# Self attention's last steps: low parts of the first context's tiles ahead of y's statistics, and four splits of W_kvc three steps later

## The chip, the cores and the metric

The kernel runs on one core of one Trainium2 chip. TensorE (PE), VectorE (DVE), ScalarE (ACT), GpSimd (POOL) and SyncE (SP) each work through an instruction stream of their own and meet at semaphores. The metric is the device time of one execution in microseconds (us); the median of several executions is compared.

## The reference, cut to what matters

It is one transformer block with cross attention, for 16 batches of 224 tokens of width 512 in 16 heads, and a context of 750 tokens for each batch:

```python
qkv = modulate(_ln(x), shift_a, scale_a) @ W_qkv + b_qkv
x = x + gate_a[:, None] * (softmax(q @ k^T * scale) @ v) @ W_proj + b_proj   # self attention, gate on all of the projection
q_c = _ln(x) @ W_qc + b_qc
kv_c = _ln(context) @ W_kvc + b_kvc
k_c, v_c = jnp.split(kv_c, 2, axis=-1)
x = x + (softmax(q_c @ k_c^T * scale) @ v_c) @ W_cproj + b_cproj             # cross attention
x = x + gate_m[:, None] * mlp(modulate(_ln(x), shift_m, scale_m))
```

(The attention lines are abridged: heads, transposes and the place of the bias are left out.)

## The kernel before, in words

Three phases follow each other: self attention (up to about 764 us of the profiled execution), cross attention (to about 1.8 ms) and the MLP. A product with full precision is made of three products of halves: every operand is split into a high part (rounded, `_h`) and a low part (the rest, `_l`), and `product` (lines 72 to 74) multiplies low by high, high by low and high by high. A split so takes two instructions: ACT writes the high part (a copy that rounds), and then DVE subtracts it from the source to get the low part.

Self attention is a software pipeline. `bodies` calls each engine's `body` for batches 0 to 16 (16 only drains what is left), and in each body `h` runs over 16 steps. Each engine has its own list of work for a step, written out by hand in the order in which the lines of its loop stand. Nothing is scheduled at run time: an engine takes its instructions in that order and waits at each semaphore that isn't there yet. PE's step has scores of one head (`score`, and `score_t` of the head six steps back), then fill work (projections for other batches), then P.V and its sums (`pv`, `sums`) and transposes (`turn_x`, `turn_y`, `turn_context`).

The last 32 steps, counted by `seam_step(b, h) = (b.c - 15) * 16 + h` (0 to 15 are batch 15's, 16 to 31 the drain's; NH is 16), also start the cross attention of its first batch, so that PE has work:

- `load_wkv` loads the weight W_kvc in eight chunks of 128x512 (four for v, four for k). `high_wkv(i)` on ACT (line 1101, tile cross_wkv_h) and `low_wkv(i)` on DVE (line 873, tile cross_wkv_l) split chunk i, ACT one step ahead of DVE. The steps are in the table `WKV_AT`.
- The context of batch 0 is six tiles of 125 tokens. At the steps of `TILES_AT` PE turns tile t (`turn_context`, line 702), ACT writes its high part (`high_context`, line 1113) and DVE its low part (`low_context`, line 895, tile cross_cT_l).
- `cross_v(t)` on PE at the steps `V_AT` (15 to 20) multiplies tile t with the v half of W_kvc. It waits for the low part of its tile, and for the four v chunks.
- `cross_k(i)` at the steps `K_AT` makes k. The first is at step 21 (NH + 5), in bank sc_ps, and begins with

```python
if i == 0:
    pe.wait_ge(wkv_l, 2 * KC)
```

  so it waits for the low parts of all eight chunks.
- The end of self attention goes on besides: `stats` (line 821, bn_stats of y), `rstd` on POOL (lines 1279 and 1281), `neg_mean` (line 831) and `apply_ln` on ACT (line 1096) normalize y, the residual sum; `turn_y` on PE (line 563), `highs_y` on ACT (line 1171) and `low_y` on DVE (line 866, tile self_yT_l) turn and split it. `turn_y` of batch 14 stands at steps 20 and 21, at the end of PE's step. `stats_context` (line 877) on DVE makes the statistics of the second context at step 19, and `sum_p` on POOL (line 1294) adds the two halves of each head's exponentials.

Self attention ends in a barrier (line 99): the cross phase starts on each engine when all have come to it.

Of the kernel before, what the change touches and what calls it, by code (L numbers as in the profile page):

```python
# [23 lines left out]
NH, HD = 16, 32  # L24
# [139 lines left out]
def self_phase(nc, x, cond_t, w_mod, b_mod, w_qkv, b_qkv_t, w_proj, b_proj, w_qc, b_qc_t, gates, x1, qc, mod_t,  # L164
# [3 lines left out]
    with ExitStack() as ctx:  # L168
# [143 lines left out]
        INVERSE_AT, MEAN_AT = (6, NH + 5), (7, NH + 7)  # L312
        NORMAL_AT = ({7: (0,), 8: (1,), 9: (2,), 10: (3,), 11: (4, 5)}, {NH + 11: (0, 1, 2), NH + 12: (3, 4, 5)})
        TILES_AT = {12: (0,), 13: (1,), 14: (2, 3), 15: (4, 5)}
        WKV_AT = (9, 10, 11, 12, 14, 15, NH, NH + 1)
        V_AT = {15: 0, NH: 1, NH + 1: 2, NH + 2: 3, NH + 3: 4, NH + 4: 5}
        K_AT = {NH + 5: 0, NH + 7: 1, NH + 8: 2, NH + 12: 3, NH + 13: 4, NH + 14: 5, NH + 15: 6}
        KEEP_K_AT = {NH + 6: 0, NH + 9: 1, NH + 10: 2, NH + 12: 3, NH + 13: 4, NH + 14: 5, NH + 15: 6}
# [5 lines left out]
        def seam_step(b, h):  # L324

            return (b.c - (B - 1)) * NH + h

        def early_division(step):

            return step >= -2 and step != 2  # L330
# [8 lines left out]
        def fills(b, h, kinds):  # L339
            if b.c in END:  # L340
                return [(kind, c, part, Batch(o)) for kind, c, part, o in END[b.c][h] if kind in kinds]
            return [(*f, b.plus(of(f))) for f in FILL[h] if f[0] in kinds and exists(b, f)]
# [19 lines left out]
        def tile_bank(o, t):  # L362

            return (st_ps + sc_ps)[t % 4] if o else pj_ps[t % 2]
# [452 lines left out]
        def _(dve):  # L817
# [11 lines left out]
            def neg_mean(b, mv, rs, nm, s_rstd, s_nmr):  # L829
                dve.wait_ge(s_rstd, b.n(1, 1))  # L830
                dve.scalar_tensor_tensor(out=nm[:], in0=mv[:, :, 0], scalar=-1.0, in1=rs[:], op0=ALU.mult, op1=ALU.mult).then_inc(s_nmr, 1)
# [58 lines left out]
            def low_context(o, t):  # L890
                at = slice(t * SN, (t + 1) * SN)
                if o == 0 and t == 0:
                    dve.wait_ge(turned, NH * (B - 1))
                dve.wait_ge(seam.cT_h, o * ST + t + 1)
                dve.tensor_tensor(seam.cT[1][:, :, at], tile_bank(o, t)[:, 0:KC * SN].rearrange("p (k n) -> p k n", k=KC),
                                  seam.cT[0][:, :, at].bitcast(F32), ALU.subtract).then_inc(seam.cT_l, 1)
# [15 lines left out]
            def split_maxima(b, g):  # L912
                turned = tx_ps[0:HPG * QT, 0:QN]
                dve.wait_ge(m_ps, b.n(KC, g + 1))
                wait(dve, m_in, b.n(32 * KC, 32 * g))
                dve.tensor_copy(mrow[0][:], turned).then_inc(m_h, 1)
                dve.wait_ge(m_h, b.n(KC, g + 1))
                dve.tensor_tensor(mrow[1][:], turned, mrow[0][:].bitcast(F32), ALU.subtract).then_inc(m_row, 1)
# [9 lines left out]
            def evict(kind, c, part, o):  # L928
                if kind == "k" and part == 1:
                    lows(o, c, k_h, k_l, bqkv, KC + 2 * c, nat)  # L930
                if kind == "q" and part == 1:
                    lows(o, c, q_h, q_l, bqs, 2 * c, natq)
                if kind == "c" and part == 1:
                    lows(o, c, c_h, c_l, bqcs, 2 * c, natq)
                if kind == "p" and part == 1:
                    add_bias(o, c)

            def body(b, att, nxt, prv, old):
                z, y2, far_b = b.plus(-1), b.plus(-2), b.plus(2)
                for h in range(NH):  # L940
                    if h % HPG == HPG - 1 and att:
                        split_maxima(b, h // HPG)
                    for f in fills(b, h, "kqcpv")[0:1]:
                        evict(*f)
                    if h < NH - 1 and att:
                        row_max(b, h + 1)
                    if h == NH - 1 and nxt:
                        row_max(b.plus(1), 0)
                    for f in fills(b, h, "kqcpv")[1:]:
                        evict(*f)  # L950
                    for _, c, _, o in fills(b, h, ("tx",)):
                        modulate(o, c)
                    for _, c, _, o in fills(b, h, ("ty",)):
                        low_y(o, c)
                    for back in (1, 2):
                        for o, g in late_group(b, h - back, att, prv) if early_division(seam_step(b, h - back)) == (back == 1) else ():
                            normalize(o, g)
                    if h == 14 and att:
                        low_o(b, 0)
                    if h in LOW_O and prv:  # L960
                        low_o(z, LOW_O[h])
                    if seam_step(b, h) in KEEP_K_AT:
                        low_k(KEEP_K_AT[seam_step(b, h)])
                    if far(b) and h == 6:
                        stats(far_b, x_in, x_loaded, lambda t: far_b.n(16, 0), st1, mv1, stats1, mvs1)
                    if far(b) and h == 8:
                        neg_mean(far_b, mv1, rs1, nm1, rstd1, nmr1)
                    if prv and h == (12 if b.c == B else 15):
                        stats(z, y, summed, lambda t: z.n(2, t + 1), st2, mv2, stats2, mvs2)
                    if old and h == 0:  # L970
                        neg_mean(y2, mv2, rs2, nm2, rstd2, nmr2)
                    if b.c == B and h == 13:
                        neg_mean(z, mv2, rs2, nm2, rstd2, nmr2)
                    if b.c == 0 and 2 <= h < 2 + KC:
                        low_w(3 * KC + h - 2)
                    if b.c == 1 and h == 0:
                        gate_rows(3)
                    if b.c == 1 and h in (13, 14):
                        mlp_row(h - 9)
                    if b.c == 1 and h == 15:  # L980
                        keep_modulation()
                    if b.c == 2 and 5 <= h < 5 + KC:
                        low_w(4 * KC + h - 5)
                    if seam_step(b, h) in WKV_AT:
                        low_wkv(WKV_AT.index(seam_step(b, h)))
                    for t in TILES_AT.get(seam_step(b, h), ()):
                        low_context(0, t)
                    for o in range(2):
                        for t in STATS_AT[o].get(seam_step(b, h), ()):
                            stats_context(o, t)  # L990
                        if seam_step(b, h) == max(STATS_AT[o]):
                            aggregate_context(o)
                        if seam_step(b, h) == MEAN_AT[o]:
                            neg_mean_context(o)
# [98 lines left out]
        def _(act):  # L1093
# [103 lines left out]
            def body(b, att, nxt, prv, old):  # L1197
                z, y2 = b.plus(-1), b.plus(-2)
                for h in range(NH):
# [28 lines left out]
                    for t in TILES_AT.get(seam_step(b, h), ()):  # L1228
                        high_context(0, t)
                    if seam_step(b, h) + 1 in WKV_AT:  # L1230
                        high_wkv(WKV_AT.index(seam_step(b, h) + 1))
                    if seam_step(b, h) == NH:
# [1554 lines left out]
```

## Time and profile before

| | |
|---|---|
| Time, median of 3 executions | 2610.44 us (2610.37 to 2615.86) |
| Profiled execution, its own time | 2611.72 us |
| Its span on the profile | 2609.9 us |
| PE busy | 2571.6 us, 99% of the span |
| DVE busy | 1695.0 us, 65% |
| ACT busy | 1127.6 us, 43% |
| POOL busy | 1274.4 us, 49% |

The span is what the profile covers; the execution's own time is 1.8 us longer. A matmul's row in the profile lasts longer than the matmul keeps its successor waiting, since matmuls are pipelined: how fast PE works is read from the distance between the starts of two matmuls, not from their durations. The same holds in small for DVE and ACT, whose rows overlap the next by some 0.08 us.

### The profile page before, as it was taken

To read this page: it belongs to the slowest core of one execution; us is meant where nothing else is said; L and a number is where in the kernel's file an instruction comes from. 1 tells how busy PE (TensorE), PEld (TensorE's weight loads), DVE (VectorE), ACT (ScalarE), POOL (GpSimd) and SP (SyncE) were. 2 spreads that over 40 slices of the span, in tenths; PEclk is the share of its full clock that TensorE was granted. 3 is DMA by queue.
4 is the path that set the end of the run, shared out by engine and by line. 5 is a ranking of instruction groups with operands and counts; after the bars stand their busy time and mean duration, and the time that the engine had idled before them with its cause. 6 is when DMAs were issued, how large, how long until landed. Compare 5 with 4: busy or idle time off the path is not lost.

```text
span 2609.9 us, 50236 instructions
## 1 busy us (share of the span) xinstructions
PE 2571.6 (99%) x18696; PEld 2127.4 (82%) x18696; DVE 1695.0 (65%) x3399; ACT 1127.6 (43%) x2192; POOL 1274.4 (49%) x1426
## 2 busy tenths in 40 slices
PE   8999999999899999999999999999899999999999
PEld 6688888888788888888888888887678888888887
DVE  6677777777767777777777777776764444444442
ACT  4354454444535555555555555554542222212111
POOL 1445454454536777777777777775421121220230
PEclk9999999999999999999999999999899999999999
DMA  7554545555554444444444444433521111111110
GB/s 224 133 134 125 136 120 131 129 125 133 146 147 114 122 107 118 112 111 117 112 117 108 123 117 109 122 95 101 150 93 45 37 45 34 44 49 37 45 53 17
DMA packets 193045, 269.89 MB, mean 103 GB/s; under 512 B 34788, under 2 KB 112612, under 8 KB 192788
## 3 DMA queue, kind: packets, MB, share of 16 engines
q1 hardware_dynamic: 187116, 254.16, 36.9%
q0 software_dynamic: 3264, 7.92, 0.9%
q10 hardware_dynamic: 2424, 4.61, 0.7%
q8 instruction: 150, 2.46, 0.4%
q14 instruction: 91, 0.75, 0.1%
HBM read 111.11 MB, written 36.77 MB: 57 GB/s over the span
## 4 chain that ended last, share of the span: by engine, by line
PE 69%; DVE 1%; issue 0%; DMA 0%; ACT 0%; SPq 0%; DVEq 0%; ACTq 0%
PE late_sc_ps L1782 7%; PE late_or_ps L1811 5%; PE late_even_ps L72 5%; PE late_sc_ps L72 5%; PE late_even_ps L73 5%; PE late_even_ps L74 5%; PE late_sc_ps L74 5%; PE late_sc_ps L73 5%; PE shared_tr_ps L1798 4%; PE late_odd_ps L72 3%; PE late_odd_ps L74 3%; PE late_odd_ps L73 3%; PE late_tr_ps L1798 3%; PE late_odd_ps L1743 1%; PE late_tr_ps L72 1%; PE late_tr_ps L74 1%
## 5 line engine op out<-in xcount | busy, mean ns | idle before, releaser
L1970 DVE TENSOR_REDUCE cross_parts<-late_sc_ps 112x1 f32<-112x500 f32 x512 | 335.5, 663 | 219.3 <-PE late_sc_ps L1782 218.3
L2224 POOL TENSOR_TENSOR cross_part<-cross_prT 125x448 f32<-125x448 f32 x232 | 271.6, 1171 | 214.6 <-ACT cross_prT L2148 177.2
L1294 POOL TENSOR_TENSOR self_psum<-self_prT 112x224 f32<-112x224 f32 x256 | 178.3, 697 | 327.4 <-ACT self_prT L1160 318.3
L2626 ACT ACTIVATE mlp_hv<-late_sc_ps,mlp_b 128x512 f32<-128x512 f32 x112 | 77.2, 689 | 511.3 <-PE late_sc_ps L74 496.9
L2148 ACT ACTIVATE cross_prT<-shared_tr_ps 125x448 f32<-125x448 f32 x379 | 206.5, 545 | 164.3 <-PE shared_tr_ps L1798 158.3
L2226 POOL TENSOR_TENSOR cross_part<-cross_part,cross_prT 125x448 f32<-125x448 f32 x232 | 268.1, 1156 | 18.2
L1782 PE MATMUL late_sc_ps<-cross_kst,cross_qst 96*112 96x500 f32 (+1 forms) x1024 | 261.2, 336 | 3.5 <-DVE cross_parts L1970 1.7
L2148 ACT ACTIVATE cross_prT<-late_tr_ps 125x448 f32<-125x448 f32 x380 | 206.8, 544 | 109.4 <-PE late_tr_ps L1798 106.6
L2540 DVE CAST mlp_hT_h<-mlp_hv 128x512 fp32r<-128x512 f32 x112 | 57.0, 509 | 300.1 <-ACT mlp_hv L2626 300.1
L1160 ACT ACTIVATE self_prT<-self_st_ps 112x448 f32<-112x448 f32 x256 | 138.6, 542 | 167.3 <-PE self_st_ps L629 165.7
L1782 PEld LDWEIGHTS late_sc_ps<-cross_kst,cross_qst 96*112 96x112 f32 x1024 | 164.3, 178 | 18.3 <-DVE cross_parts L1970 2.6
L909 DVE TENSOR_REDUCE self_nmax<-self_sc_ps 112x2 f32<-112x448 f32 x256 | 154.7, 614 | 33.1 <-PE self_sc_ps L600 33.0
L72 PE MATMUL late_sc_ps<-mlp_xT_l,mlp_w_h 128*128 128x512 f32 x448 | 175.8, 392 | 0.0
L74 PE MATMUL late_sc_ps<-mlp_xT_h,mlp_w_h 128*128 128x512 f32 x448 | 175.1, 391 | 0.0
L73 PE MATMUL late_sc_ps<-mlp_xT_h,mlp_w_l 128*128 128x512 f32 x448 | 175.0, 391 | 0.0
L1972 DVE TENSOR_REDUCE cross_parts<-late_sc_ps 112x2 f32<-112x500 f32 x256 | 170.2, 665 | 0.0
L2228 POOL TENSOR_TENSOR cross_psum<-cross_part 125x224 f32<-125x224 f32 x232 | 155.4, 670 | 18.2
L1798 PE MATMUL shared_tr_ps<-cross_qst,cross_kst 98*125 98x224 f32 x768 | 159.4, 289 | 3.3 <-ACT cross_prT L2148 2.7
L1798 PE MATMUL late_tr_ps<-cross_qst,cross_kst 98*125 98x224 f32 x768 | 152.3, 280 | 1.8 <-ACT cross_prT L2148 1.4
L1798 PEld LDWEIGHTS shared_tr_ps<-cross_qst,cross_kst 98*125 98x125 f32 x768 | 125.0, 188 | 34.0 <-issue 12.5
L1798 PEld LDWEIGHTS late_tr_ps<-cross_qst,cross_kst 98*125 98x125 f32 x768 | 131.6, 188 | 22.0 <-ACT cross_prT L2148 8.3
L1811 PE MATMUL late_or_ps<-cross_prT,cross_vt 125*32 125x224 f32 x2784 | 143.7, 354 | 0.0
(402 smaller groups left out, 7280.0 us busy)
## 6 DMA issues: line engine op xcount, KB each, us to landing
cross_kst<-cross_nat_h SPq DMA_DIRECT2D x508, 93.8 KB, 2.2
cross_kst<-cross_nat_l SPq DMA_DIRECT2D x254, 93.8 KB, 2.2
cross_qst<-qc SPq DMA_DIRECT2D x192, 112.0 KB, 2.4
cross_c_in<-in_context SPq DMA_DIRECT2D x78, 224.0 KB
self_kst<-self_nat_h SPq DMA_DIRECT2D x128, 112.0 KB, 2.3
self_qst<-self_natq_h SPq DMA_DIRECT2D x128, 112.0 KB, 3.0
self_x_in<-in_x SPq DMA_DIRECT2D x16, 448.0 KB, 3.8
self_kst<-self_nat_l SPq DMA_DIRECT2D x64, 112.0 KB, 2.2
```

The costliest lines, as they stand in the source:

```text
L72: pe.matmul(out, lhs[0], rhs[1], start=first, stop=False)
L73: pe.matmul(out, lhs[1], rhs[0], start=False, stop=False)
L74: return pe.matmul(out, lhs[0], rhs[0], start=False, stop=last)
L1294: pool.tensor_tensor(psum[:, j], prT[:, j, 0], prT[:, j, 1], ALU.add).then_inc(p_summed, 1)
L1782: last = pe.matmul(sc_ps[u][0:QN, at:at + cn], qst[g][0:TERMS * HD, j, t * QN:(t + 1) * QN], kst[g][j][0:TERMS * HD, c0:c0 + cn], start=Tr ...
L1798: last = pe.matmul(bank(h, c)[0:SN, m * N:(m + 1) * N], kst[g][j][:, kt * SN:(kt + 1) * SN], qst[g][:, j, :], start=True, stop=True)
L1811: last = pe.matmul(or_ps[HD * j:HD * j + HD, 0:N], vt[b.par][:, kt, h * HD:h * HD + HD], prT[:, slot(h), kt], start=kt == 0, stop=kt == ST ...
L1970: dve.tensor_reduce(parts[:, g % 2, j, u, 0:1], sc_ps[u][0:QN, 0:SHALF[0]], AX_X, ALU.max, negate=True).then_inc(maxed, 1)
L1972: dve.tensor_reduce(parts[:, g % 2, j, :, 1], sc_ps[u][0:QN, 0:QT * SHALF[1]].rearrange("p (t k) -> p t k", t=QT), AX_X, ALU.max, negate=T ...
L2148: act.activation(probabilities(b, h)[:, 2 * c:2 * c + 2], bank(h, c)[0:SN, 0:2 * N].rearrange("p (k t) -> p k t", k=2), ACT.Exp).then_inc( ...
L2224: pool.tensor_tensor(part[:], prT[:, j, 0:2], prT[:, j, 2:4], ALU.add).then_inc(pre_summed, 1)
L2226: pool.tensor_tensor(part[:], part[:], prT[:, j, 4:6], ALU.add).then_inc(pre_summed, 1)
```

## The change

Two things, both in the last steps of self attention.

First, the call of `low_context(0, t)` in DVE's step moves up: ahead of y's statistics (`stats`, `neg_mean`) and of `low_wkv` of the same step, behind `low_o`. Second, `WKV_AT` gives the last four chunks of W_kvc (those of k) the steps 17 to 20 in place of 14 to 17. ACT's `high_wkv` goes with them, a step ahead: 16 to 19 in place of 13 to 16. PE's, POOL's and SP's streams are the same as before, and so are all waits.

```diff
-        WKV_AT = (9, 10, 11, 12, 14, 15, NH, NH + 1)
+        WKV_AT = (9, 10, 11, 12, NH + 1, NH + 2, NH + 3, NH + 4)
...
                     if far(b) and h == 8:
                         neg_mean(far_b, mv1, rs1, nm1, rstd1, nmr1)
+                    for t in TILES_AT.get(seam_step(b, h), ()):
+                        low_context(0, t)
                     if prv and h == (12 if b.c == B else 15):
                         stats(z, y, summed, lambda t: z.n(2, t + 1), st2, mv2, stats2, mvs2)
...
                     if seam_step(b, h) in WKV_AT:
                         low_wkv(WKV_AT.index(seam_step(b, h)))
-                    for t in TILES_AT.get(seam_step(b, h), ()):
-                        low_context(0, t)
```

On DVE, steps 15 and 16 stand as follows. `cross_cT_l` are the low parts of context tiles 4 and 5, `self_st` and `self_mv` the statistics of y, `self_nm` its negative mean, `cross_wkv_l` the low part of a chunk of W_kvc. This is before:

```order
L821 BN_STATS self_st<-self_y 112x6 x2
L824 MEMSET self_turn 1x1
L826 BN_AGGR self_mv<-self_st 112x2 x2
L873 TENSOR_TENSOR cross_wkv_l<-cross_wkv_raw,cross_wkv_h 128x512
L895 TENSOR_TENSOR cross_cT_l<-self_pj_ps,cross_cT_h 128x4x125
L895 TENSOR_TENSOR cross_cT_l<-shared_tr_ps,cross_cT_h 128x4x125
L831 SCALAR_TENSOR_TENSOR self_nm<-self_mv,self_rs 112x2
```

And this is the same place with the change:

```order
L895 TENSOR_TENSOR cross_cT_l<-self_pj_ps,cross_cT_h 128x4x125
L895 TENSOR_TENSOR cross_cT_l<-shared_tr_ps,cross_cT_h 128x4x125
L821 BN_STATS self_st<-self_y 112x6 x2
L824 MEMSET self_turn 1x1
L826 BN_AGGR self_mv<-self_st 112x2 x2
L831 SCALAR_TENSOR_TENSOR self_nm<-self_mv,self_rs 112x2
L873 TENSOR_TENSOR cross_wkv_l<-cross_wkv_raw,cross_wkv_h 128x512
```

The tiles' low parts now come first, the statistics behind them, and no split of a chunk stands between.

Steps 18 to 21 of DVE, as the difference. `self_rb` and `self_ou` are the division of a head group's output, `self_st_c` and `self_mv_c` the second context's statistics, `self_yT_l` the low part of y turned (`low_y`), at steps 20 and 21:

```order
+L873 TENSOR_TENSOR cross_wkv_l<-cross_wkv_raw,cross_wkv_h 128x512
+L923 RECIPROCAL self_rb<-self_or_ps 128x224
+L926 TENSOR_TENSOR self_ou<-self_or_ps,self_rb 128x224
+L873 TENSOR_TENSOR cross_wkv_l<-cross_wkv_raw,cross_wkv_h 128x512
 L877 BN_STATS self_st_c<-cross_c_in 125x6 x6
 L881 MEMSET self_turn 1x1
 L883 BN_AGGR self_mv_c<-self_st_c 125x2 x6
-L866 TENSOR_TENSOR self_yT_l<-self_tx_ps,self_yT_h 128x448 x2
+L866 TENSOR_TENSOR self_yT_l<-self_tx_ps,self_yT_h 128x448
+L873 TENSOR_TENSOR cross_wkv_l<-cross_wkv_raw,cross_wkv_h 128x512
+L866 TENSOR_TENSOR self_yT_l<-self_tx_ps,self_yT_h 128x448
```

The seventh chunk's split now stands between the division and the context's statistics, and the eighth's between the two parts of y.

## Rows read from the trace of the kernel before

**Rows 1.** The page: busy time by engine, and the chain that ended last.

```profile
PE 2571.6 (99%) x18696; PEld 2127.4 (82%) x18696; DVE 1695.0 (65%) x3399; ACT 1127.6 (43%) x2192; POOL 1274.4 (49%) x1426
PE 69%; DVE 1%; issue 0%; DMA 0%; ACT 0%; SPq 0%; DVEq 0%; ACTq 0%
```

**Rows 2.** Busy time in stretches of 6 us: length, engines, PE's clock, DMA.

```profile
696.00:702.00 6.00, 4.46 (x29) 3.62 (x27) 5.86 (x10) 3.40 (x7) 3.84 (x4) 1.00 0.02 5
...
720.00:726.00 6.00, 6.00 (x32) 4.89 (x32) 5.45 (x15) 1.37 (x4) 1.33 (x2) 1.00 0.00 0
...
762.00:768.00 6.00, 4.38 (x32) 4.09 (x32) 3.17 (x7) 1.26 (x4) 2.22 (x4) 1.00 0.92 222
```

**Rows 3.** Timeline of PE, first matmuls of cross_v(2) and cross_v(3): start, duration.

```profile
712.04 0.49 PE L72 MATMUL self_pj_ps<-cross_wkv_l,cross_cT_h 128*125 128x512 f32 x1
712.37 0.40 PE L73 MATMUL self_pj_ps<-cross_wkv_h,cross_cT_l 128*125 128x512 f32 x1
...
715.14 0.40 PE L72 MATMUL shared_tr_ps<-cross_wkv_l,cross_cT_h 128*125 128x512 f32 x1
715.38 0.39 PE L73 MATMUL shared_tr_ps<-cross_wkv_h,cross_cT_l 128*125 128x512 f32 x1
```

**Rows 4.** Timeline of DVE, 699 to 713 us.

```profile
699.37 1.45 DVE L873 TENSOR_TENSOR cross_wkv_l<-cross_wkv_raw,cross_wkv_h 128x512 fp32r<-128x512 f32 x1
...
701.87 0.68 DVE L873 TENSOR_TENSOR cross_wkv_l<-cross_wkv_raw,cross_wkv_h 128x512 fp32r<-128x512 f32 x1
...
709.26 1.28 DVE L821 BATCH_NORM_STATS2 self_st<-self_y 112x6 f32<-112x512 f32 x2
...
711.32 0.67 DVE L895 TENSOR_TENSOR cross_cT_l<-self_pj_ps,cross_cT_h 128x500 fp32r<-128x500 f32 x1
711.90 0.67 DVE L895 TENSOR_TENSOR cross_cT_l<-shared_tr_ps,cross_cT_h 128x500 fp32r<-128x500 f32 x1
712.49 0.51 DVE L831 SCALAR_TENSOR_TENSOR self_nm<-self_mv,self_rs 112x2 f32<-112x2 f32 x1
```

**Rows 5.** Timeline of ACT, 709 to 726 us.

```profile
709.08 0.59 ACT L1113 CAST cross_cT_h<-shared_tr_ps 128x500 fp32r<-128x500 f32 x1
...
714.12 1.51 ACT L1096 ACTIVATE self_x_res<-self_y,self_nm,self_rs 112x512 f32<-112x512 f32 x2
...
725.99 0.53 ACT L1171 CAST self_yT_h<-self_tx_ps 128x448 fp32r<-128x448 f32 x1 [2.39 <-PE self_tx_ps L563]
```

**Rows 6.** Timeline of PE around cross_k(0), 725 to 729 us.

```profile
725.35 0.55 PE L563 MATMUL self_tx_ps<-shared_ident,self_x_res 112*128 112x112 f32 x4
...
725.94 0.34 PE L72 MATMUL self_sc_ps<-cross_cT_l,cross_wkv_h 128*128 128x376 f32 x1
...
728.04 0.55 PE L563 MATMUL self_tx_ps<-shared_ident,self_x_res 112*128 112x112 f32 x4
```

**Rows 7.** Timeline of DVE, 719 to 728 us; in brackets the idle time before.

```profile
719.42 1.56 DVE L923 RECIPROCAL self_rb<-self_or_ps 128x224 f32<-128x224 f32 x1 [4.44 <-PE self_or_ps L653]
...
725.18 0.41 DVE L883 BATCH_NORM_AGGREGATE self_mv_c<-self_st_c 125x2 f32<-125x6 f32 x5
726.56 0.62 DVE L866 TENSOR_TENSOR self_yT_l<-self_tx_ps,self_yT_h 128x448 fp32r<-128x448 f32 x1 [0.96 <-ACT self_yT_h L1171]
```

**Rows 8.** Timeline of POOL, two instructions beside DVE's.

```profile
698.99 1.28 POOL L1302 TENSOR_TENSOR self_y<-self_y,self_gate 112x512 f32<-112x512 f32 x1
...
727.53 0.67 POOL L1294 TENSOR_TENSOR self_psum<-self_prT 112x224 f32<-112x224 f32 x1 [3.18 <-ACT self_prT L1160]
```

**Rows 9.** Timeline of PE: first matmul behind the barrier.

```profile
765.82 0.45 PE L1782 MATMUL late_sc_ps<-cross_kst,cross_qst 96*112 96x500 f32 x1 [1.62 <-PEq L99]
```

**Rows 10.** Busy time in stretches of 2 us, columns as in rows 2.

```profile
674.00:676.00 2.00, 0.58 (x4) 0.27 (x2) 2.00 (x5) 1.21 (x3) 1.66 (x3) 1.00 1.03 257
676.00:678.00 2.00, 1.01 (x4) 0.66 (x4) 1.90 (x3) 0.50 (x1) 0.02 (x1) 0.55 1.08 309
...
682.00:684.00 2.00, 2.00 (x17) 1.91 (x14) 1.96 (x11) 0.55 (x1) 0.37 (x1) 0.74 0.20 73
```

## The prediction

> **What bounds the kernel now.** I read the page first: PE is busy for 2571.6 us, 99% of the span, and has 69% of the chain that ended last, all other engines together about 1% [rows 1]. So an edit on DVE and ACT is worth only what it gives PE, or takes from it, in time between two matmuls. The change touches steps 12 to 20 of the seam, so I read next the stretches of 6 us there [rows 2]: from 696 to 702 us PE has 4.46 of 6 us, from 720 to 726 it is full, and from 762 to 768 it has 4.38. The first hole lies ahead of everything that the change moves (step 12 starts with the addition that ends this hole); the last is the barrier at the end of the phase. In between PE is full by the stretches. Since busy rows hide short waits, I then read the timelines for starts: PE at each product that waits for a low part [rows 3, 6], and DVE and ACT beside it [rows 4, 5, 7].
>
> **First part: tiles ahead of the statistics.** It adds and removes nothing; DVE does the same work in another order. Who waits for a tile's low part is cross_v(2), which needs five tiles. Before, tile 4's low part starts at 711.32 and takes 0.67, so it ends at 711.99 [rows 4], and cross_v(2) has its first matmul at 712.04, 0.05 us later, and its second 0.33 us after that; for cross_v(3), which waits for nothing, the distance is 0.24 us [rows 3]. So the wait shows, and is worth about 0.1 us (0.33 - 0.24 = 0.09). With the change tile 4 no longer stands behind the statistics and a split. Tile 5's high part on ACT starts at 709.08 and ends at 709.67 [rows 5], tile 4's stands right ahead of it, so the low part of tile 4 is there by about 709.9 and that of tile 5 by 709.67 + 0.04 + 0.67, some 710.4 to 710.5. That is 2 us ahead of cross_v(2): the wait is gone, **-0.1 us**. I take 0 to -0.3 as bounds: 0 if the distance of 0.33 has another cause, -0.3 if an earlier step of PE also waits a little for a low part that comes 0.6 us sooner (one split less ahead of it, from here 0.58 us of DVE).
>
> What is late next is y's negative mean. From the start of its statistics to its own start DVE took 712.49 - 709.26 = 3.23 us [rows 4], POOL's two instructions included. The statistics now start at about 710.4, so the negative mean starts at about 713.65 and ends, with 0.51, near 714.15. Behind it on DVE waits the fifth chunk's split, which nobody needs before step 21. On ACT the normalization of y waits for it; that one started at 714.12 because ACT had other work until then [rows 5], so it is late by nothing to 0.2 us. Turned y is wanted by PE only at 725.35 [rows 6], ten microseconds on. I cost this at nothing; if the cover were gone, it would be 1.2 us (713.65 - 712.49), the whole shift.
>
> **Second part: four splits three steps later.** On ACT four copies (about 0.6 us each, as the cast of a tile in rows 5) leave steps 13 to 16 and enter steps 16 to 19. ACT is busy for 1.37 of 6 us between 720 and 726 [rows 2]; nothing on PE gets late from that. On DVE four splits of 0.68 us [rows 4] leave steps 14 to 17. Three of them go to steps 17 to 19: two into the 4.44 us that DVE idles before 719.42 [rows 7], and one behind the division, which shifts the second context's statistics by some 0.6 us. Their end moves from 725.18 + 0.41 = 725.59 to about 726.2, still ahead of 726.56, where DVE idled 0.96 us for y's high part [rows 7]. Cost nothing, with 0.3 us of cover.
>
> The fourth is the one that costs. It stands at step 20 behind `low_y`, and cross_k(0), the first work of PE at step 21 behind `score_t`, waits for all eight low parts. The chain ahead of it is fixed by PE itself: y is turned from 725.35, ending 725.90 [rows 6]; ACT's high part follows at 725.99 for 0.53 [rows 5]; DVE's low part at 726.56 for 0.62 [rows 7]; the next DVE instruction starts 0.58 after its start, as the two tiles in rows 4 do after each other, so the split runs from 727.14 to 727.82; PE follows 0.05 later, as in rows 3 and 4: 727.87. Before, cross_k(0) started at 725.94 [rows 6], with all splits long done. The wait is 727.87 - 725.94 = **+1.93 us**, a new hole in a stretch where PE had none. Behind it in PE's stream are cross_k(0) itself, the second half of y's turn (728.04 before, about 729.9 then), P.V of the last head group and everything up to the barrier; what DVE and ACT do there follows PE and moves with it. PE has no hole between 726 us and the barrier in which to give the time back, and at the barrier the 1.62 us [rows 9] are spent after the last arrival, which is PE's own. So the hole is carried to the end in full.
>
> Bounds of the hole: 1.7 us, if DVE and PE each answer 0.1 us faster than in these rows; 2.7 us, if the split is held up by POOL as the one at 699.37 was, 1.45 in place of 0.68 us while POOL worked on y from 698.99 to 700.27 [rows 4, 8]. Here POOL's next instruction starts at 727.53 [rows 8], 0.4 us after the split has started, so I take the short duration. The Trainium skill (SBUF — State Buffer, "SBUF: two separate sides") says that a VectorE operation with two SBUF inputs and a GpSimd operation that reads SBUF exclude each other, and that whichever starts first keeps the ports for its whole length. By that rule the split keeps its 0.68 us and the sum on POOL waits some 0.3 us; the rows of the split at 699.37 agree with it.
>
> **The sum.** -0.1 + 1.93 is +1.8 us. Against the profiled execution (2609.9 us span, 1.8 us around it, 2611.72 in all) that is 2613.5 us. That execution was 1.3 us above the median of the runs shown (2610.44), so for a median I expect 2610.44 + 1.8 = 2612.2 us, 0.07% more. A measurement of this kernel can't tell less than about 0.2% (5.2 us) from no change: the likeliest verdict is no difference, with a small sign to the slower side. The runs shown spread from 2610.37 to 2615.86 with nothing changed, which is more than the effect.
>
> **Rivals.**
> 1. *The hole is hidden* (0.06). Either PE's wait at step 21 doesn't come last, or a later wait gives the time back. For it: only one PE wait in a phase is moved, and DVE has 4.44 us of idle time before 719.42 [rows 7]. Against it: that lies ahead of the split's place in DVE's stream, which is bound behind `low_y`, and PE's stretches from 726 on are full. It would give -0.1 us: 2610.3.
> 2. *The hole is longer* (0.12): the context's statistics run late (their loads land later, or the seventh split is held up), `low_y` starts behind them, and the eighth split with it; or POOL comes first. The price is up to 0.8 us for each of the two splits (1.45 - 0.68), less the 0.3 us of cover for the seventh: +1.8 + 0.8 + 0.5 = +3.1 at most, 2613.5.
> 3. *Slower, by the clock* (0.07). Where PE had only 0.58 of 2 us (674 to 676), its clock fell in the next stretch (mean 0.55, from 2.4 to 1.2 GHz for most of it) and came back inside the stretch from 682, whose mean is 0.74 [rows 10]: some 1.8 + 4 + 1.0 = 6.8 us at 1.2 GHz, which in dense work is 3.4 us lost. A hole of 1.9 us at 726 could do the same. Against it: two holes nearly as long (1.54 us within 696 to 702, and 1.62 at the barrier) left the mean at 1.00 [rows 2, 9]. It decides if the clock falls at the new hole and stays down for those 6.8 us, since all of the work behind it is dense: +1.8 + 3.4 = +5.2 us, 2615.6 to 2616 us, the edge of slower.
> 4. *Faster by over 0.2%* (0.02). It would need the clock to stay up in a stretch where it now falls (such as 676 to 683, 3.4 us) and the hole to be hidden as well. Nothing that the change does touches those stretches.
>
> **How the numbers follow.** The forecast has 0.73, rival 1 0.06, rival 2 0.12, rival 3 0.07, rival 4 0.02. The forecast's own range is 2610.44 + 1.4 to + 2.6 (hole 1.7 to 2.7, less 0.3 to 0), with the spread of a median around it. The range for 8 in 10 leaves out most of rivals 1, 3 and 4 and holds what repeated executions vary by on both sides: 2609.9 to 2615.4. Within 0.2% lie the forecast, rivals 1 and 2 and some of rival 3, 0.93; slower is most of rival 3, 0.05; faster is rival 4, 0.02.
>
> **What the changed profile would show.** PE's cross_k(0) starts at about 727.8, with 1.8 to 2 us of idle time ahead, put down to DVE's cross_wkv_l at line 873; the split ahead of it lasts 0.68 us and stands right behind `low_y`. cross_v(2)'s first two matmuls are 0.24 us apart, not 0.33. Tile 5's low part ends near 710.5, y's normalization on ACT starts within 0.3 us of 714.12, and the second half of y turned is at about 729.9. From there to the barrier every distance is as before, and PE's clock is 1.00 from 700 to 764. The prediction is wrong if PE has no idle time before cross_k(0), if the time between cross_k(0) and the barrier shrinks, or if a stretch at 1.2 GHz follows the hole.

## The result, and the profile after

Over 22 executions of each kernel, the changed kernel has a median of 2614.52 us (2611.38 to 2618.32), the one before 2610.89 us (2606.29 to 2616.41). The ratio is 1.0014, with a 95% interval of 1.0009 to 1.002: slower by 3.7 us, with an interval from 2.3 to 5.2 us. That lies inside the range (2609.9 to 2615.4), and within 0.2% as forecast, but it is twice the 1.8 us of the sum. Two executions far outside all others, 4281.79 us of the kernel before and 3475.23 us of the kernel with the dense delay of 2.0 us, are left out of every mean below. The profiled execution took 2614.62 us; its page begins:

```profile
span 2612.8 us, 50236 instructions
PE 2572.5 (98%) x18696; PEld 2128.8 (81%) x18696; DVE 1694.6 (65%) x3399; ACT 1126.2 (43%) x2192; POOL 1273.2 (49%) x1426
```

Against [rows 1], the span is 2.9 us longer. PE's busy time has grown by 0.9 us (2572.5 against 2571.6) with the same 18696 matmuls, and the time in which it isn't busy by 2.0 us (40.3 against 38.3): PE waits more, and some of its work has become slower. The timeline of PE where rows 6 were read (start, duration, and in brackets the idle time before and who ended it):

```profile
725.73 0.55 PE L563 MATMUL self_tx_ps<-shared_ident,self_x_res 112*128 112x112 f32 x4
726.04 0.44 PE L629 MATMUL self_st_ps<-self_qst,self_kst 98*112 98x224 f32 x2
728.30 0.41 PE L72 MATMUL self_sc_ps<-cross_cT_l,cross_wkv_h 128*128 128x376 f32 x1 [1.82 <-DVE cross_wkv_l L873]
...
730.45 0.55 PE L563 MATMUL self_tx_ps<-shared_ident,self_x_res 112*128 112x112 f32 x4
```

The hole is where it was forecast, and the trace names the tile that PE waits for, cross_wkv_l. From the turn of y to cross_k(0) there are 2.57 us (728.30 - 725.73), and there were 0.59 [rows 6]: 1.98 us more. The chain in front of it, on ACT and DVE:

```profile
726.36 0.53 ACT L1171 CAST self_yT_h<-self_tx_ps 128x448 fp32r<-128x448 f32 x1 [2.39 <-PE self_tx_ps L563]
```

```profile
726.93 0.62 DVE L866 TENSOR_TENSOR self_yT_l<-self_tx_ps,self_yT_h 128x448 fp32r<-128x448 f32 x1 [0.36 <-ACT self_yT_h L1171]
727.47 0.68 DVE L873 TENSOR_TENSOR cross_wkv_l<-cross_wkv_raw,cross_wkv_h 128x512 fp32r<-128x512 f32 x1
```

DVE's idle time before `low_y` has shrunk from 0.96 [rows 7] to 0.36 us: that is the seventh split, hidden with 0.36 us to spare. The eighth runs from 727.47 to 728.15 with nothing to hide it.

The second place that differs is behind the barrier. Busy time in stretches of 2 us (length, PE, PEld, DVE, ACT, POOL, PE's clock as a share of 2.4 GHz, DMA), first of the changed kernel, then of before:

```profile
766.00:768.00 2.00, 0.62 (x6) 0.43 (x4) 0.00 (x0) 0.00 (x0) 0.00 (x0) 1.00 1.00 321
768.00:770.00 2.00, 1.76 (x8) 1.69 (x9) 1.35 (x4) 0.79 (x2) 1.80 (x3) 0.76 1.06 225
770.00:772.00 2.00, 2.00 (x8) 1.90 (x7) 1.81 (x4) 0.00 (x0) 0.92 (x2) 0.50 1.10 244
772.00:774.00 2.00, 2.00 (x13) 1.95 (x12) 0.91 (x3) 0.57 (x1) 0.00 (x0) 0.89 1.12 231
```

```profile
764.00:766.00 2.00, 0.38 (x3) 0.23 (x3) 0.09 (x1) 0.20 (x1) 0.22 (x1) 1.00 1.08 308
766.00:768.00 2.00, 2.00 (x12) 1.86 (x12) 1.69 (x3) 0.59 (x2) 2.00 (x4) 1.00 1.04 245
768.00:770.00 2.00, 2.00 (x13) 1.95 (x13) 2.00 (x6) 0.57 (x1) 0.50 (x1) 1.00 1.12 219
```

The barrier's hole is 1.62 us in both. In the changed kernel the clock falls to 1.2 GHz behind it: 0.24, 0.50 and 0.11 of three stretches of 2 us are missing, 1.7 us of clock. Two of its stretches hold x8 matmuls each, where before they held x12 and x13. Before, the clock stays up.

Since the two PE streams are the same, each matmul's start can be set against the same matmul's start before. The difference, worked out from the two traces, at some times of the kernel before:

```
at (us of before)     690   703   708   720   727.9   763   766   780   1800   1845   1888   end
after - before (us)  0.38  0.38  0.48  0.37   2.41   2.41  2.42  3.95   3.54   2.03   2.89   2.91
```

The 0.38 stands there before the change begins. Then come 2.04 us between 720 and 727.9, not one hundredth between there and 763 us, and 1.53 us behind the barrier. During cross attention 0.4 us of the difference go away. What follows between 1800 and 1888 are stretches at 1.2 GHz at the start of the MLP. They are cut up differently from profile to profile, but in each of the fourteen profiles of this document they add up to the same 13.7 us. Here their place gives 0.6 us back from 1800 us to the end (3.54 to 2.91), so this pair of profiles differs by less than the hole and the slow stretch together.

### The profile page after: what moved, and what is told of

It reads as the page before. It is cut to its first block, busy times and chain, and to the rows that moved or that the text cites. A ratio compares the mean times of both kernels' runs of the same rounds, so it can differ in the third digit from the quotient of the medians.

```text
span 2612.8 us, 50236 instructions
## 1 busy us (share of the span) xinstructions
PE 2572.5 (98%) x18696; PEld 2128.8 (81%) x18696; DVE 1694.6 (65%) x3399; ACT 1126.2 (43%) x2192; POOL 1273.2 (49%) x1426
## 4 chain that ended last, share of the span: by engine, by line
PE 69%; DVE 1%; issue 0%; DMA 0%; ACT 0%; SPq 0%; DVEq 0%; ACTq 0%
PE late_sc_ps L1782 7%; PE late_or_ps L1811 5%; PE late_even_ps L72 5%; PE late_sc_ps L72 5%; PE late_even_ps L74 5%; PE late_even_ps L73 5%; PE late_sc_ps L74 5%; PE late_sc_ps L73 5%; PE shared_tr_ps L1798 4%; PE late_odd_ps L72 3%; PE late_odd_ps L74 3%; PE late_odd_ps L73 3%; PE late_tr_ps L1798 3%; PE late_odd_ps L1743 1%; PE late_tr_ps L72 1%; PE late_or_ps L1820 1%
```

## The experiments

Twelve runs, each beside executions of the kernel before: nine edited kernels, one of them measured twice, and the changed kernel and the one before once more. All medians are of 11 executions (6 for "the hole lengthened"). They were measured in three groups; the kernel before has medians of 2611.58, 2610.64 and 2610.78 us there, over 28 to 33 executions. At the end a table has all of them together.

**The second part alone.** The kernel before with

```diff
-        WKV_AT = (9, 10, 11, 12, 14, 15, NH, NH + 1)
+        WKV_AT = (9, 10, 11, 12, NH + 1, NH + 2, NH + 3, NH + 4)
```

> The kernel before with the second part alone: the four chunks of k split at steps 17 to 20, the tiles' low parts where they were. Theory H (the whole systematic cost is the hole in front of cross_k(0)): the hole is there, PE idle 1.8 to 1.9 us before its first matmul, cross_v(2) still or no longer loses its 0.1 us, and from the turn of y at step 20 to the barrier PE takes 2.0 us longer than before; the median is 2 us above before's, give or take 1. Theory C (the clock takes part: the later barrier or the hole brings a stretch at 1.2 GHz behind it): the same hole, but a median 3 to 5 us above, with a stretch at 1.2 GHz behind the barrier in the profile. Theory T (moving the tiles is part of the cost): about 1.5 us less than the whole change cost, so near the size of the hole or below.

Measured: 2615.14 us, ratio 1.0013 (1.0004 to 1.0022). PE waits for the same split, and as long:

```profile
728.25 0.41 PE L72 MATMUL self_sc_ps<-cross_cT_l,cross_wkv_h 128*128 128x376 f32 x1 [1.82 <-DVE cross_wkv_l L873]
```

and its clock falls behind the barrier as in the changed kernel:

```profile
768.00:770.00 2.00, 1.80 (x7) 1.70 (x8) 1.39 (x4) 0.79 (x2) 1.84 (x3) 0.67 1.06 227
770.00:772.00 2.00, 2.00 (x7) 1.91 (x7) 1.55 (x4) 0.00 (x0) 0.87 (x2) 0.50 1.12 234
```

So the steps of the four splits are the whole cost, as far as 11 executions can tell (in the mean 3.8 us above before, the whole change 3.6), and it is not the hole alone.

**The first part alone.** The changed kernel with `WKV_AT` as before.

> The first part alone: the tiles' low parts ahead of the statistics, the chunks at their old steps. Theory H: no hole at cross_k(0), PE's first two matmuls of cross_v(2) 0.24 us apart in place of 0.33, the median within 1 us of before's, by -0.1 us if it could be seen. Theory C: the same, and no stretch at 1.2 GHz between 700 us and the MLP's start. Theory T: 1 to 2 us slower, with a wait of PE between 700 and 715 us that before doesn't have.

Measured: 2611.27 us, ratio 1.0003 (0.9994 to 1.0012), no hole, no stretch at 1.2 GHz between 700 us and the MLP. cross_v(2)'s first two matmuls are 0.24 us apart (712.81 and 713.05). Moving the tiles costs and brings nothing that can be measured; theory T, by which it costs 1 to 2 us with a new wait, is out by the trace: PE's only wait there is the one that before has too, 1.54 us.

**One step sooner.** The changed kernel with

```diff
-        WKV_AT = (9, 10, 11, 12, NH + 1, NH + 2, NH + 3, NH + 4)
+        WKV_AT = (9, 10, 11, 12, NH, NH + 1, NH + 2, NH + 3)
```

> The changed kernel with the four chunks at steps 16 to 19 in place of 17 to 20: the last split then stands ahead of the second context's statistics at step 19, not behind the low part of y. Theory H: no idle time before cross_k(0), all of the 2 us gone, median within 1 us of before's (-0.1 us). Theory C: the same unless the clock falls behind the barrier by itself. A third theory (late splits load VectorE whatever their step) would leave over 1 us of idle time somewhere between 715 and 730 us.

Measured: 2609.49 us, ratio 0.9998 (0.9989 to 1.0007), and once more at the end of the study:

> e3 once more, for a second profile and a narrower comparison. Theory H: no idle time before cross_k(0), PE's distance from the first matmul of cross_v(0) to the first behind the barrier 60.65 us, no stretch at 1.2 GHz between 700 us and the end of the cross phase, and a median within 1 us of before's.

with 2610.75 us, ratio 1.0004 (0.9995 to 1.0013). The first median is 2.1 us below the one of before in its group, more than the 1 us that I had allowed, and the second agrees with its own to 0.03 us: two medians of the same kernel differ by 1.3 us here. There is no idle time before cross_k(0) in either profile. This is DVE of the first, steps 19 and 20:

```profile
720.47 0.68 DVE L873 TENSOR_TENSOR cross_wkv_l<-cross_wkv_raw,cross_wkv_h 128x512 fp32r<-128x512 f32 x1
721.07 3.65 DVE L877 BATCH_NORM_STATS2 self_st_c<-cross_c_in 125x6 f32<-125x512 f32 x6
...
725.63 0.62 DVE L866 TENSOR_TENSOR self_yT_l<-self_tx_ps,self_yT_h 128x448 fp32r<-128x448 f32 x1 [0.36 <-ACT self_yT_h L1171]
```

All four splits are still two steps later than before, and the hole is gone: what counts is the place of the last one behind `low_y`, not that splits are late.

**The hole lengthened.** The changed kernel, with four more instructions in front of the last split:

```diff
+        idle = sb("idle", [SN, 4, 6])
...
                 dve.wait_ge(wkv_h, i + 1)
+                for r in range(4 if i == 2 * KC - 1 else 0):
+                    dve.bn_stats(idle[:, r], wkv[0][0:SN, k, at].bitcast(F32))
```

> The changed kernel with four more instructions on VectorE ahead of the last split (statistics of a 125x512 piece of a weight, into an unused tile; about 0.61 us each, 2.4 us in all; results are the same). Theory H: the idle time before cross_k(0) goes from 1.8 to 4.3 us and all of it arrives at the barrier and at the end: median 2.0 + 2.4 = 4.4 us above before's. Theory C: more than that, 6 us or more, with a stretch at 1.2 GHz behind the hole or behind the barrier. If something later gives time back, less than 4 us.

Measured: 2616.77 us, ratio 1.0029 (1.0017 to 1.004), which is 4.4 to 10.4 us above before. That does not separate the 4.4 us of theory H from the 6 of theory C; the profile does. PE idles 4.19 us, near the 4.3 expected, and the clock falls right behind:

```profile
726.00:728.00 2.00, 0.00 (x0) 0.00 (x0) 2.00 (x5) 0.00 (x0) 1.84 (x3) 1.00 0.00 0
728.00:730.00 2.00, 1.47 (x6) 1.50 (x7) 0.38 (x1) 0.00 (x0) 0.12 (x1) 0.74 0.00 0
730.00:732.00 2.00, 2.00 (x8) 1.97 (x7) 0.00 (x0) 0.00 (x0) 0.00 (x0) 0.50 0.00 0
732.00:734.00 2.00, 2.00 (x30) 1.20 (x28) 0.58 (x2) 1.15 (x3) 0.00 (x0) 0.91 0.18 22
```

From its first matmul of cross_v(0) to the first behind the barrier PE takes 5.84 us longer than before (66.57 against 60.73): 4.3 us of hole and 1.5 us of slow clock. Behind the barrier the clock stays up this time. The lengthening arrives in full at the barrier, and with it the clock's share.

**The changed kernel and the one before, again.**

> The changed kernel once more, for a second profile. Theory C (the change brings a stretch at 1.2 GHz behind the barrier in many executions): the stretch is there again between 766 and 774 us, mean clock about 0.9942, median 3.2 to 3.6 us above before's. Theory H (the hole alone, the rest is chance): no such stretch, and a median nearer to 2 us above before's.

> The kernel before once more, for a second profile and as a measure of chance: median within 0.7 us of before's, PE's distance from the first matmul of cross_v(0) to the first behind the barrier 60.7 us again. Theory C: no stretch at 1.2 GHz between 700 us and the end of the cross phase. Theory H: it may be there or not.

Measured: 2614.11 us, ratio 1.0013 (1.0004 to 1.0022), for the changed kernel, and 2612.32 us, 1.0001 (0.9992 to 1.0011), for the one before. The changed kernel's second profile has the same idle time of 1.82 us before cross_k(0), but the slow stretch is not behind the barrier. It is behind the hole:

```profile
728.00:730.00 2.00, 0.34 (x2) 0.37 (x3) 1.22 (x2) 1.20 (x3) 0.73 (x1) 0.97 0.00 0
730.00:732.00 2.00, 2.00 (x8) 2.00 (x7) 0.00 (x0) 0.00 (x0) 1.58 (x3) 0.50 0.00 0
732.00:734.00 2.00, 2.00 (x14) 1.78 (x16) 0.00 (x0) 0.01 (x1) 0.00 (x0) 0.68 0.00 0
```

So my expectation named the wrong place, and the cost is the same. What I had named as a sign that the prediction is wrong, a stretch at 1.2 GHz behind the hole, is there in this profile. In numbers: hole and stretch together are 3.50 us there (64.23 against 60.73 us from cross_v(0) to behind the barrier), of which 1.5 us is the clock's. Before's second profile has none between 700 us and the MLP. Its median, though, is 1.7 us above that of the 33 executions beside it, where I had allowed 0.7 (in the mean 0.8 us above them): so far apart can two medians of one kernel lie. The mean clock doesn't repeat either: 0.9947 for the changed kernel, where I expected 0.9942, and 0.9945 for the one before.

**A delay without idle time.** The kernel before, with four products more ahead of cross_k(0), so that PE is late but busy:

```diff
                     pe.wait_ge(wkv_l, 2 * KC)
+                for _ in range(4 if i == 0 else 0):
+                    product(pe, k_bank(i)[:, 0:cn], tuple(w[:, 0, g * P:(g + 1) * P] for w in wkv),
+                            tuple(c[:, 0, c0:c0 + cn] for c in seam.cT), True, True)
```

> The kernel before, with four further products (12 matmuls of 376 columns, 0.17 us each, 2.06 us) in front of cross_k(0), whose result is overwritten: PE reaches the barrier 2 us later as in the changed kernel, but without idle time. Theory P (the clock behind the barrier depends only on when PE gets there): a median as far above before's as the changed kernel's, 3.2 to 3.6 us, a mean granted clock over the executions of 0.9942 as there, and in some profiles a stretch at 1.2 GHz behind the barrier. Theory I (the idle time itself takes clock): 2.1 us above before's and a mean granted clock of 0.9948 as before's.

Measured: 2615.23 us, or 2614.65 us over the ten executions without the one at 3475.23 us; ratio 1.0014 (1.0005 to 1.0023), as much as the changed kernel, though PE has no hole in front of cross_k(0); 2.04 us are the added work. The mean clock is 0.9946, between the two expectations. In the profile the clock falls behind the barrier:

```profile
768.00:770.00 2.00, 0.38 (x3) 0.27 (x2) 0.09 (x1) 0.27 (x1) 0.29 (x1) 1.00 1.07 295
770.00:772.00 2.00, 2.00 (x9) 1.89 (x8) 1.75 (x3) 0.52 (x2) 2.00 (x4) 0.63 1.07 229
772.00:774.00 2.00, 2.00 (x7) 1.91 (x7) 1.50 (x4) 0.00 (x0) 0.43 (x1) 0.52 1.10 222
```

Theory I, by which the new idle time itself takes the clock, does not explain this: for a slow stretch behind the barrier a later arrival is enough. For the stretches right behind the hole (the changed kernel again, the hole lengthened) there is no run without the idle time at that place, so they may be its doing.

**Other delays.** The same kernel with seven products (3.6 us) and with two (1.0 us) in place of four.

> The kernel before with seven further products in front of cross_k(0) in place of e6's four (21 matmuls, 3.6 us of dense work, results overwritten). Theory P (what the clock does behind the barrier depends on when PE gets there, and in no simple order): it need not fall there, since the barrier's hole comes 1.5 us later than in the changed kernel; if it does not, the median is 3.6 us above before's, no more than the changed kernel's 3.4 although the delay is 1.6 us longer. Theory Q (any later arrival brings the stretch at 1.2 GHz): 5.1 us above, with the stretch in the profile. Theory R (a delay costs its own length and the rest was chance): 3.6 us.

> The kernel before with two further products in front of cross_k(0) (6 matmuls, 1.03 us of dense work). Theory P: the stretch at 1.2 GHz behind the barrier may already be there, and the median then is 2.5 us above before's. Theory Q: the same, 2.5 us. Theory R: 1.0 us, and no stretch behind the barrier in the profile.

Measured: 2614.73 us, ratio 1.0016 (1.0007 to 1.0025), with 3.6 us of work, and 2613.85 us, 1.0011 (1.0003 to 1.002), with 1.0 us. Neither profile has a slow stretch behind the barrier; of the longer delay:

```profile
768.00:770.00 2.00, 1.63 (x15) 1.44 (x13) 0.86 (x2) 0.00 (x0) 0.00 (x0) 1.00 0.84 213
770.00:772.00 2.00, 0.75 (x5) 0.68 (x5) 0.34 (x2) 0.77 (x2) 0.79 (x2) 1.00 1.09 245
772.00:774.00 2.00, 2.00 (x14) 1.96 (x13) 2.00 (x5) 0.02 (x1) 1.93 (x3) 1.00 1.03 268
```

The times don't decide between the theories. In the mean the delays of 1.0, 2.0 and 3.6 us cost 2.4, 3.6 and 4.5 us (each with a standard error of 0.5 to 0.7 us), and 4.5 lies between the 3.6 of P and R and the 5.1 of Q. The profile with 3.6 us speaks against Q, and so does its mean clock of 0.9949, no lower than before's. With 1.0 us the profile has no slow stretch, but over the eleven executions the mean clock is lower than before's by 0.0009. Taken over all executions within each kernel, 0.001 of mean clock goes with 1.5 us, so a slower clock would account for 1.3 us, which with the 1.0 of work is the 2.4 measured. Where in those executions the clock was down, one profile doesn't tell.

**Two tries to gain from the hole near 700 us.** Before the change PE waits 1.54 us there for an addition behind the split that takes 1.45 us in place of 0.68 beside POOL [rows 2, 4, 8]. First, on top of "one step sooner", v's third and fourth chunk at other steps:

```diff
-        WKV_AT = (9, 10, 11, 12, NH, NH + 1, NH + 2, NH + 3)
+        WKV_AT = (9, 10, 12, 14, NH, NH + 1, NH + 2, NH + 3)
```

> The kernel e3 (tiles first, chunks of k at steps 16 to 19) with the third and fourth chunk of v split at steps 12 and 14 in place of 11 and 12. In before's trace the third chunk's split runs from 699.37 for 1.45 us beside POOL's product of y, and the addition that frees PE's bank stands behind it: PE waits 1.54 us for that addition. Theory H (a hole of PE counts in full, wherever it is): the hole near 700 us shrinks from 1.5 to 0.2 us or less, nothing else gets late (the fourth chunk's split is there when cross_v(0) comes to its fourth chunk), and the median is 1.3 us below e3's, about 1.5 us below before's. Rival: the addition or another instruction of VectorE takes over the wait (or cross_v(0) waits for its fourth chunk), and the gain is under 0.5 us.

Measured: 2610.68 us, ratio 1.0 (0.9991 to 1.0008). PE's wait falls to 0.19 us, and much of that is given back behind it:

```profile
699.85 0.62 PE L702 MATMUL shared_tr_ps<-shared_ident,cross_c_in 125*128 125x125 f32 x4 [0.19 <-DVE self_y L857]
...
702.39 0.59 PE L653 MATMUL self_or_ps<-self_psum,self_ones 112*32 112x224 f32 x8 [0.61 <-POOL self_psum L1294]
```

The sums now wait for POOL, and cross_v(0) loses another 0.3 us at its fourth chunk. Of 1.36 us, 0.48 are left at 720 us, of which the tiles' earlier low parts have 0.1. The rival was right. Second, the split in the same step but ahead of the division:

```diff
+                    if seam_step(b, h) == 11:
+                        low_wkv(WKV_AT.index(11))
                     for back in (1, 2):
...
-                    if seam_step(b, h) in WKV_AT:
+                    if seam_step(b, h) in WKV_AT and seam_step(b, h) != 11:
```

> e3 (tiles first, chunks of k at steps 16 to 19) with the split of v's third chunk at step 11 moved ahead of the division, where POOL has not yet started its product of y: the split should take 0.7 us in place of 1.45, and the addition behind the division end 0.7 us sooner. If PE's hole near 700 us counts in full it shrinks from 1.5 to 0.8 us and the median is 0.7 us below e3's and about 1 us below before's. Rival: the later division holds up something else on PE (the sums, or POOL's product of y and through it the next sums), as in e5, and nothing is gained.

Measured: 2609.36 us, ratio 0.9998 (0.9989 to 1.0007), the lowest median of the study, but not to be told from before's. The trace shows what it does: the split takes its short time, PE's wait is halved (0.78 us in place of 1.54), and 0.21 us of the gain go to the sums. By 720 us PE is 0.6 us ahead of before.

```profile
695.86 0.67 DVE L873 TENSOR_TENSOR cross_wkv_l<-cross_wkv_raw,cross_wkv_h 128x512 fp32r<-128x512 f32 x1
```

```profile
699.24 0.62 PE L702 MATMUL shared_tr_ps<-shared_ident,cross_c_in 125*128 125x125 f32 x4 [0.78 <-DVE self_y L857]
701.38 0.59 PE L653 MATMUL self_or_ps<-self_psum,self_ones 112*32 112x224 f32 x8 [0.21 <-POOL self_psum L1296]
```

**All together.** "Distance" is from PE's first matmul of cross_v(0) to its first behind the barrier, in the profile; "slow" is where PE ran at 1.2 GHz between 700 and 1800 us; mean and clock are over the executions (changed: 33, one step sooner: 22; before: the 104 of the experiments, since no clock is on record for the 22 of the result, whose mean is 2611.11 us).

```
kernel                      distance          slow            mean us   clock
before                      60.73 and 60.78   nowhere, twice  2610.98   0.99496
changed                     62.67 and 64.23   barrier; hole   2614.54   0.99436
second part alone           62.68             barrier         2614.79   0.99400
first part alone            60.61             nowhere         2611.39   0.99482
one step sooner             60.65 and 60.61   nowhere, twice  2610.37   0.99536
hole lengthened             66.57             hole            2617.51   0.99417
dense delay 2.0 us          62.77             barrier         2614.56   0.99460
dense delay 3.6 us          64.32             nowhere         2615.51   0.99491
dense delay 1.0 us          61.76             nowhere         2613.37   0.99409
chunks at 12 and 14         60.95             nowhere         2610.32   0.99491
split ahead of division     60.64             nowhere         2609.85   0.99536
```

One order in the slow stretches can be read from these traces, after the fact and without a run that tests it. Counted from the start of the span, PE's first matmul behind the barrier stands at 768.24 us in the changed kernel, with a slow stretch, and at 767.85 us in before's second profile, without one: the time since the start decides nothing. But every profile has an earlier slow stretch, which ends between 681 and 686 us (near 683 in [rows 10]). Counted from its end, that matmul comes after 84.5 to 84.9 us in the three profiles with a slow stretch behind the barrier, after 82.0 to 83.4 us in eight without one (both of before among them, and the delay of 1.0 us), and after 85.7, 85.8 and 88.8 us in three more without (changed again, the delay of 3.6 us, the hole lengthened). The barrier's hole is equally long in all fourteen, so in these profiles it was its place behind the last slow stretch, and not its length, that went with the loss of clock.

## Why the prediction was right, and where it was too small

- **The hole**: forecast 1.93 us, measured 1.98. Its place, the tile waited for and the order of the chain are as written: y turned, high part, low part, split, PE. The durations of 0.53, 0.62 and 0.68 us came back unchanged. That the sum is right to 0.05 us is in part luck: the split started 0.54 us behind the low part and not 0.58, and PE followed 0.15 us behind the split (728.15 to 728.30) and not 0.05.
- **The split keeps its 0.68 us**: right. The sum on POOL beside it, which started at 727.90 in the changed profile, took 0.76 us in place of 0.67. That is the direction of the lock between VectorE and GpSimd that the Trainium skill states (SBUF — State Buffer, "SBUF: two separate sides"), but of the 0.3 us of waiting that I worked out from it only 0.09 came. The two rows overlap by 0.25 us, and other overlaps of these two traces fall short in the same way: the split beside POOL's product [rows 4, 8] was lengthened by 0.77 us where 0.90 overlap, a sum on POOL at 702.02 us behind a split by 0.38 where 0.53 overlap. The wait is 0.13 to 0.16 us shorter than the overlap of the rows.
- **cross_v(2) wins 0.1 us**: right, 0.24 us between its first matmuls in place of 0.33. The second part alone does it as well (712.46 and 712.70), so the wait was for a tile behind one split too many, and either move ends it. What I left out is that the split at step 12, which now starts behind a sum on POOL and not ahead of it, took 0.79 us in place of 0.68, and a turn of a tile waited 0.1 us for the low part behind it: the difference in the table goes from 0.38 to 0.48 and back to 0.37. The first part comes to nothing, not to -0.1 us.
- **Three splits are free, with 0.3 us of cover**: right; 0.36 us of idle time were left.
- **The statistics of y are late by 1.2 us and nobody waits**: right in what matters, y was turned when PE came to it. The negative mean started at 713.59 in place of 712.49, 1.1 us later. But the normalization on ACT, which I had nothing to 0.2 us late, started sooner, at 713.79 in place of 714.12: of the two copies of a chunk that ACT makes ahead of it, at 709.55 and 710.98 us, one had moved to a later step. I had counted the copies that leave, and not that the normalization gains by it.
- **Carried in full to the barrier and the end**: right for the barrier, to 0.01 us, in the first profile. Behind it the step fails: "at the barrier the 1.62 us are spent after the last arrival", and so nothing would change there. The length of the barrier's hole is the same, but what PE's clock does behind it is not.
- **The term that was missing** is that stretch at 1.2 GHz, 1.53 us in the profile. I had it as rival 3, with 0.07, at 3.4 us and behind the new hole only. I gave two reasons against it, the holes of 1.54 and 1.62 us that leave the clock at 1.00 [rows 2, 9]. The step that failed is the inference from them: the same hole of 1.62 us, reached 2 us later, does lose the clock, and in the second profile of the changed kernel the clock fell right behind the new hole of 1.82 us, as rival 3 had it. A hole that leaves the clock alone in one profile is no proof that it does so at another time. The price was too high as well, since I took the stretch of 6.8 us in rows 10 for the rule, and the stretches here are half as long.
- **The size**: 2.0 us of hole and 1.5 us of slow clock make 3.5 us, and 3.6 us were measured (means 2614.54 and 2610.98, each sure to some 0.2 to 0.3 us). The clock's part is less sure over many executions than in the profiles. The mean clock is lower by 0.0006. With the 1.5 us that go with 0.001 of clock within each kernel, that accounts for 0.9 us; counted by stretches, one of 3.4 us at half clock lowers the mean clock of an execution by 0.00065, so nearly every execution would have had one, and they would account for 1.4 us (an estimate). Nearly all of that drop is in the first 22 executions (0.9942); the eleven later ones have 0.9947.
- **The range**: the forecast's own range was 2611.8 to 2613.0 us, and the median of 2614.52 lies above it. It lies within the range for 8 in 10 only by what I had added for the spread of repeated executions, not by a term for this stretch. That is luck.

What is shown: the hole and its cause, by the kernel with the second part alone, the one a step sooner and the one with the hole lengthened. A slow stretch was in each of the five profiles in which PE came to the barrier 1.9 to 2.0 us late or had the new hole (changed twice, second part alone, hole lengthened, dense delay of 2.0 us), and in none of the other nine. That such a stretch belongs to most executions of the changed kernel is made likely by the mean clock and not shown. What stays open is how often each place is hit, and where the clock is down in the executions with the dense delay of 1.0 us; one profile for a kernel doesn't tell it.

## What to carry to other kernels

Before a preparation is moved later, look for its last reader and for what stands ahead of it in the new place: three of the four splits were free, and the fourth cost 2 us only because it stood behind an instruction that itself waits for PE, one step before PE asks for it. On an engine that is full up to the next barrier, a wait of that kind arrives there undiminished, and its price can have a second part, since a hole or a shifted barrier can take the clock down for some microseconds (3.4 us here, worth 1.5). A move that brings 0.1 us in one wait is worth less than the run-to-run spread, so the trace is what tells whether it did anything.

## What the runs showed of the hardware

- PE's clock fell to 1.2 GHz behind the barrier's hole of 1.62 us in three of fourteen profiles: those in which PE got there 1.9 to 2.0 us later than before, counted from cross_v(0), whether it had been idle on the way (changed kernel, second part alone) or busy (dense delay). It did not fall in the eight in which PE got there up to 1.0 us later or no later, nor in the three in which it was 3.5 us later or more. The same hole of 1.82 us in front of cross_k(0) was followed by a slow stretch in one profile and not in two others (changed kernel, second part alone).
- Each of the five slow stretches between 700 and 1800 us lasted 3.4 us and cost about 1.5 us, a little under half of its length: behind the barrier seven or eight matmuls start in 2 us of such a stretch, against thirteen.
- At the start of the MLP the stretches at 1.2 GHz add up to 13.7 us in each of the fourteen profiles, in two or three pieces.
- The 104 executions of the kernel before took 2605.86 to 2614.58 us. Taken over all executions, within each kernel, 0.001 of mean granted clock went with 1.5 us of time.
